# Trainium2 case: VectorE readouts one scan later, ScalarE's side work behind the decays, the D term by transposes, and three GpSimd pairs in the last quarter

## What is computed

```python
xz = einsum('bsd,ed->bse', xn, in_proj_w);  x_in, z = split(xz, 2)
u  = silu(conv4(x_in) + conv_b)                    # 1024 inner channels
dt_r, B, C = split(u @ x_proj_w.T, [64, 80]);  dt = softplus(dt_r @ dt_proj_w.T + b)
# for each token t, state n of 16:
h  = h * exp(dt_t * A) + (dt_t * u_t) * B_t
y  = einsum('bdn,bn->bd', h, C_t)
y  = (y + u * D_param) * silu(z);  out = x + gate * (y @ out_proj_w.T)
```

## Time and profile before

| | |
|---|---|
| time, median of 3 runs | 4975.43 us (4974.64 to 4975.75) |
| the profiled execution's own time | 4976.74 us |
| its span, first to last instruction | 4975.0 us |
| busy, share of the span | PE 89%, DVE 83%, ACT 63%, POOL 81% |
| mean granted TensorE clock | 0.976 of 2.4 GHz |
| first and last `dbu` of GpSimd (L635) | 113.8 and 3733.8 us |

### The profile page before, as it was taken

The page is one execution under the profiler, slowest core; times in us unless marked ns, Lnnn a source line. Parts: engine busy times, 40 slices in busy tenths (PEclk is TensorE's granted clock), DMA queues, the critical chain, the costliest instruction groups (busy, mean ns, idle before and its releaser), DMA issues. The chain is left out here.

```text
span 4975.0 us, 74942 instructions
## 1 busy us (share of the span) xinstructions
PE 4419.1 (89%) x21856; PEld 3161.0 (64%) x21856; DVE 4137.6 (83%) x5011; ACT 3129.7 (63%) x7557; POOL 4010.7 (81%) x1861
## 2 busy tenths in 40 slices
PE   7898888888898989888888888898976999999998
PEld 4666666666666666666666666666654666565664
DVE  2999999999999999999999999999993656566664
ACT  2777777777777777777777777777761333333332
POOL 0999999999999999999999999999992333334332
PEclk9999999999999999999999999999988999999999
DMA  5111111111111111111111111111103323222221
GB/s 193 39 43 46 43 46 43 44 52 52 62 46 44 46 44 46 44 43 44 54 57 58 43 44 46 44 46 43 43 35 112 101 84 100 84 100 79 97 87 45
DMA packets 121581, 301.58 MB, mean 61 GB/s; under 512 B 15394, under 2 KB 20770, under 8 KB 120675
## 3 DMA queue, kind: packets, MB, share of 16 engines
q1 hardware_dynamic: 121186, 296.91, 17.6%
HBM read 245.35 MB, written 51.51 MB: 60 GB/s over the span
## 5 line engine op out<-in xcount | busy, mean ns | idle before, releaser
L635 POOL TENSOR_TENSOR dbu<-du,bc 128x1024 f32<-128x1024 f32 x1024 | 2406.8, 2383 | 111.2 <-DVE du L573 111.2
L396 ACT ACTIVATE dA<-dt,c_A 128x256 f32<-128x256 f32 x4096 | 1753.5, 467 | 524.4 <-DVE hC L539 392.4
L602 DVE TENSOR_TENSOR_SCAN hS<-dA,dbu 128x512 f32<-128x512 f32 x1024 | 1205.4, 1208 | 176.1 <-PE Y L277 123.6
L646 POOL TENSOR_TENSOR hS<-hS,bc 128x1024 f32<-128x1024 f32 x512 | 1220.0, 2383 | 62.7 <-DVE hS L602 62.7
L602 DVE TENSOR_TENSOR_SCAN dA<-dA,dbu 128x512 f32<-128x512 f32 x1024 | 1208.5, 1212 | 20.8 <-ACT dA L396 15.0
L277 PEld LDWEIGHTS Y<-c_ident,hC 128*128 128x128 f32 x4096 | 481.0, 144 | 284.6 <-DVE hC L539 190.2
L277 PE MATMUL Y<-c_ident,hC 128*128 128x128 f32 x4096 | 556.2, 280 | 116.1 <-DVE hC L539 112.1
L539 DVE TENSOR_TENSOR hC<-dA,bc 128x1024 f32<-128x1024 f32 x512 | 627.0, 1225 | 22.4 <-DVE dA L602 5.7
L318 PE MATMUL side<-c_in_w,xnF 128*128 128x512 f32 x1024 | 509.1, 621 | 94.0 <-DVE u L565 55.5
L277 PE MATMUL Y<-c_ident,hS 128*128 128x128 f32 x4096 | 548.9, 278 | 16.1 <-POOL hS L646 16.1
L335 PE MATMUL side<-xnF,c_in_w 128*128 128x256 f32 x2048 | 491.4, 384 | 73.8 <-DVE zs L560 49.1
(11 more groups left out here) (125 smaller groups left out, 5668.5 us busy)
## 6 DMA issues: line engine op xcount, KB each, us to landing
bc<-b_scratch SPq DMA_DIRECT2D x256, 512.0 KB, 3.8
x_in<-in_x SPq DMA_DIRECT2D x32, 512.0 KB, 5.2
o_scratch<-oS SPq DMA_DIRECT2D x64, 256.0 KB, 2.0
p_o_in<-o_scratch SPq DMA_DIRECT2D x32, 512.0 KB, 4.8
p_g_in<-gate_scratch SPq DMA_DIRECT2D x32, 512.0 KB, 5.8
p_x<-in_x SPq DMA_DIRECT2D x32, 512.0 KB, 6.4
x_scratch<-p_x_in SPq DMA_DIRECT2D x32, 512.0 KB, 3.2
p_xr<-x_scratch SPq DMA_DIRECT2D x32, 512.0 KB, 6.8
```

Of the source, the lines that this page charges most:

```text
L396: last = act.activation(dA[:, q % A_RING, e, :], dt[j % 2][:, e, :], ACT.Exp, scale=C["A"][:, 2 * j + e, n:n + 1])
L602: dve.tensor_tensor_scan(out.rearrange("p e t -> p (e t)"), dA[:, q % A_RING, :, :].rearrange("p e t -> p (e t)"), dbu[(q // 2) % B_RING][ ...
L635: gps.tensor_tensor(dbu[p % B_RING][:, :, :, :], du[j % 2][:, :, :].unsqueeze(1).broadcast_to([P, 2, 2, GT]), bc[:, 0, n:n + 2, :].unsquee ...
L646: gps.tensor_tensor(h, h, bc[:, 1, n:n + 2, :].unsqueeze(2).broadcast_to([P, 2, 2, GT]), ALU.mult).then_inc(hcP_done, 1)
```

## The change

It has eight parts.

1. `KINDS` becomes a list by quarter. Quarters 0 to 2 stay GGDGDGDD; quarter 3 becomes GDGDDGDD. A group then has 15 G pairs and 17 D pairs in place of 16 and 16. The slots are still given in turn modulo three, now written out as tables.
2. VectorE reads out a D pair one scan later, behind the first scan of the next pair (`t = 16 * j + 2 * p + 2`).
3. ScalarE goes two units at a time: all four decays of a pair, then the side work of both units.
4. The skip term: ScalarE computes u * D into a new SBUF tile `uD` (`skip_values`, two activations in a quarter, at `UD_AT`), and TensorE adds it by four transposes with the identity. The diagonal matrix and its eight instructions in setup go.
5. The `du` product (L573) is taken out of VectorE's DT step and moved from four units after TensorE's DT piece to five; the copy of dt from six to seven.
6. The XN activations are split in two halves, two units apart; XI copies go from two to three units behind.
7. The sigmoid stages stay one unit apart, and the tables `SIDE`, `D_ACC`, `G_ACC`, `YZ_AT`, `YT_AT`, `YF_AT`, `DMM_AT` and the layer norm's places are new. `YF_AT` of quarter 1 (37) is now below its `YT_AT` (38).
8. VectorE's u product waits for `uD_done` in place of `dmm_done`.

```diff
-KINDS = "GGDGDGDD"
+KINDS = ["GGDGDGDD", "GGDGDGDD", "GGDGDGDD", "GDGDDGDD"]
-D_ACC = [8, 11, 15, 17]
-G_ACC = [7, 10, 14, 17]
+D_ACC = {4: [9, 12, 16, 18], 5: [9, 10, 12, 16, 18]}
+G_ACC = {4: [8, 10, 14, 17], 3: [8, 12, 17]}
@@
-    ("XI", 2, 1, [7, 8, 8, 9]),
-    ("O", 0, -1, [9, 10, 12, 13, 13, 14, 14, 15]),
-    ("CV", 1, 1, [16, 16, 18, 18]),
+    ("XI", 2, 1, [9, 10, 11, 11]),
+    ("O", 0, -1, [10, 11, 11, 11, 12, 12, 13, 14]),
+    ("CV", 1, 1, [15, 15, 16, 17]),
@@
-    ("CV", 0, 2, [57, 58, 59, 60]),
+    ("CV", 0, 2, [57, 59, 60, 61]),
@@
-A_AFTER = {"Z": 2, "CV": 2, "DT": 2, "XN": 2, "XI": 2, "XP": 2, "O": 2}
-DT_COPY = 6
+A_AFTER = {"Z": 2, "CV": 2, "DT": 2, "XN": 2, "XI": 3, "XP": 2, "O": 2}
+S1 = 1
+S2 = 2
+DU_AFTER, DT_COPY = 5, 7
-YZ_AT = [18, 34, 50, 66]
-YT_AT = [20, 36, 52, 68]
-YF_AT = [22, 38, 54, 70]
-DMM_AT = [6, 22, 38, 54]
-Q_STATS, Q_AGGR, Q_RSTD, Q_NMR, Q_XHAT = 34, 35, 38, 40, 42
+YZ_AT = [19, 35, 51, 67]
+YT_AT = [20, 38, 53, 69]
+YF_AT = [23, 37, 56, 70]
+DMM_AT = [8, 24, 40, 56]
+UD_AT = [1, 17, 33, 49]
+Q_STATS, Q_AGGR, Q_RSTD, Q_NMR, Q_XHAT = 29, 31, 34, 34, 38
@@ TensorE, skip_term
-            wait(pe, u_done, g * 4 + (j + 1))
+            wait(pe, uD_done, g * 4 + (j + 1))
-                    last = pe.matmul(Y[:, b, k * P:(k + 1) * P], u[par][:, 2 * j + k, b * P:(b + 1) * P],
-                                     W["skip"][:, 2 * j + k, :], start=(b == 0 and k == 0), stop=False, skip_group_check=True)
+                    last = pe.matmul(Y[:, b, k * P:(k + 1) * P], uD[:, k, b * P:(b + 1) * P], C["ident"][:, :],
+                                     start=(b == 0 and k == 0), stop=False, is_transpose=True, skip_group_check=True)
@@ ScalarE
+        def skip_values(g, j, par):
+
+            wait(act, u_done, g * 4 + (j + 1))
+            wait(act, dmm_done, g * 4 + j)
+            for k in range(2):
+                last = act.activation(uD[:, k, :], u[par][:, 2 * j + k, :], ACT.Copy, scale=C["dcol"][:, 2 * j + k:2 * j + k + 1])
+            last.then_inc(uD_done, 1)
@@
+            for q in range(0, UNITS, 2):
+                if inside(at, 0):
+                    for i in range(2):
+                        bank_freed(act, g, q + i)
+                        if q % NST == 0 and i == 0:
+                            wait(act, dtc_done, g * 4 + (q // NST + 1))
+                        decay(g, q + i, 0)
+                        decay(g, q + i, 1)
+                beside(q)
+                beside(q + 1)
@@ VectorE
-                    if KINDS[p] == "D" and half == 1:
-                        readout(g, j, D_PAIRS.index(p))
                 for j in range(4):
+                    for m, p in enumerate(D_PAIRS[j]):
+                        t = 16 * j + 2 * p + 2
+                        if q == t % UNITS and inside(at, -(t // UNITS)):
+                            readout(g - t // UNITS, j, m)
@@ setup
-        for e in range(KI):
-            dve.tensor_scalar(W["skip"][:, e, :], C["ident"][:, :], C["dcol"][:, e:e + 1], None, ALU.mult)
```

More of the change, by code:

```diff
@@ L102 @@
 S_RING = 3
+C_SLOT = [i % C_RING for i in range(ND)]
+S_SLOT = [(G_BASE[j] + i + sum(j >= at for at in (1, 3)[:-NGP % S_RING])) % S_RING for j in range(4) for i in range(len(G_PAIRS[j]))]
 PAIRS = UNITS // 2
@@ L398, in decay, with simple @@
                 last.then_inc(dA_ready, 1)
-        def simple(kind, j, src, own, par):
+        def simple(kind, j, src, own, par, part):
             wait(act, filled[kind], nth(kind, j, own))
@@ L404, in simple @@
                 wait(act, filled["Z"], own * 4 - 4)
[L405 to L410, removed]
+                for b in range(GB):
+                    k, s = 2 * j + part, (part * GB + b) * P
+                    last = act.activation(xnF[par][:, k, b * P:(b + 1) * P], src[:, s:s + P], ACT.Identity,
+                                          scale=C["gm0"][:, bass.ds(own * GB + b, 1), k], bias=C["bm0"][:, bass.ds(own * GB + b, 1), k])
+                if part == 1:
+                    last.then_inc(xn_done, 1)
             elif kind == "XI":
@@ L480, in stages, with beside @@
                         staged(kind, j, stage, bank[bk], tmp[(sig_base[of] + s) % 2], go + d, earlier(2, s, of, go, sigs_at))
[L482 to L491, removed]
+            def beside(q):
+                stages(q, 2, S2)
+                stages(q, 1, S1)
                 stages(q, 0, 0)
@@ L495, in body @@
                         copy_dt(j, bank[bk], go + d)
-                    if kind in ("XN", "XI", "XP", "O") and q == end + A_AFTER[kind] - off:
-                        simple(kind, j, bank[bk], go + d, (of + d) % 2)
+                    for part in range(2 if kind == "XN" else 1):
+                        if kind in ("XN", "XI", "XP", "O") and q == end + A_AFTER[kind] + 2 * part - off:
+                            simple(kind, j, bank[bk], go + d, (of + d) % 2, part)
                 for j in range(4):
+                    if q == UD_AT[j] and inside(at, 0):
+                        skip_values(g, j, at % 2)
                     t = YF_AT[j]
@@ L561, in side_dve @@
             elif kind == "CV":
-                wait(dve, dmm_done, own * 4 - 8 + (j + 1))
+                wait(dve, uD_done, own * 4 - 8 + (j + 1))
                 wait(dve, filled["XP"], own - 1)
@@ L619, in body @@
                 for (kind, j, d, end, bk, s, off), of, go in side:
+                    if kind == "DT" and q == end + DU_AFTER - off:
+                        step_times_u(j, bank[bk], go + d, (of + d) % 2)
                     if kind in D_AFTER and q == end + D_AFTER[kind] - off:
@@ L652, in body @@
                 for j in range(4):
[L653 to L654 removed]
+                    for m in range(len(G_PAIRS[j])):
+                        t = 8 * j + G_PAIRS[j][m] + G_LAG
                         if p == t % PAIRS and inside(at, -(t // PAIRS)):
@@ L1255, in program @@
             for name, shape in (("in", [P, KD, 2 * DI]), ("x", [P, KI, XD]), ("dt", [XD + 1, DI]),
-                                ("out", [P, KI, D]), ("conv", [P, KI, TAPS, P]), ("skip", [P, KI, P])):
+                                ("out", [P, KI, D]), ("conv", [P, KI, TAPS, P])):
                 const(layer0, W, name + "_w", shape)
```

111 lines of the change are left out of this document (56 added, 55 removed).

## The result

The changed kernel takes 4927.17 us (median, 4924.26 to 4930.41), the kernel before on the same chip 4975.59: ratio 0.9902, 95% interval 0.9885 to 0.9919, so 48 us less. I had forecast 109 us less, 4866. The time lies in my range of 4836 to 4935, near its upper end.

What follows compares the result with a forecast made beforehand. GpSimd was taken as the bound; after the change it needs 109.0 us a group, VectorE 108.8. With 0.9 for unevenness the group takes 110.0; with setup 109.4 us less, 4866 by the median, range 4836 to 4935.

Steps and rivals of the forecast that it cites:

- GpSimd's work: GpSimd's readouts: one fewer a group, 47 instructions in place of 48 at 2.319 us, 74.2 us less work.
- All of it on the path: GpSimd sets the pace, so the 74.2 us of work it loses all come off the kernel's time.
- The boundary wait: First G pair of a group: VectorE's 123.6 us of waits for TensorE's transposes go; 0.85 us a group of jump gap comes.
- ScalarE's waits for decays: VectorE's scans waiting for ScalarE's decays: taken as unchanged at 1.6 us a group, bounds 0 and 5.
- The split XN: XN activations split in halves on ScalarE: said to have units of slack and costed at nothing.
- `take_y` of quarter 1: On ScalarE, ahead of TensorE's turn in order: the place to watch, within the unchanged 1.6 us a group.
- Skip term: ScalarE gains 4 us a group, TensorE saves 2 with no gain in time; price zero, from 0 to 4 us a group.
- Late readout: VectorE's readout one scan later: saves 1.1 us busy time a group; slack before the needing scan falls from 1.24 to 0.10 us.
- my rival on the slower side: Late decays at the scan behind each readout cost 6.2 us a group, some 5025 us; chance of slower 0.12.
- GpSimd's remaining waits: Unevenness of GpSimd and VectorE in turn: 0.9 us a group, 28.8 us in all, where 62.7 are now.
- Setup: VectorE loses 1.65 us of work at setup's end; 1.3 us less time taken, bounds 0 and 1.65.
- VectorE becomes the bound: Rival: slack behind a readout missed in some D pairs, 2.4 us a group, 111.2 a group, around 4904 us; chance 0.17.

Runs made afterwards that it cites:

- the mended one: The changed kernel with XN emptied whole again, two units behind TensorE, and take_y of quarter 1 at unit 39 in place of 37: 4851.03 us, ratio 0.9744.
- four bodies: The changed kernel with XN whole and take_y at 39, plus four bodies in the hardware loop in place of two: 4854.08 us, ratio 0.9756.
- whole XN: The changed kernel with ScalarE emptying an XN bank in one go again, not in two halves two units apart: 4863.12 us, ratio 0.9774.
- the kernel with ScalarE's old order: The kernel before with 15 G and 17 D pairs, TensorE's places for them and the readout one scan later, ScalarE's order as before: 5133.71 us, ratio 1.0313.
- its variant with the matmuls: The changed kernel with XN whole and take_y at 39, skip term by four float32 matmuls with the diagonal matrix, no uD: 4894.25 us, ratio 0.9833.
- the old division: GGDGDGDD in all four quarters, 16 G and 16 D pairs: 4918.45 us in the changed kernel, 4916.06 us with XN whole and take_y at 39.

## Why the prediction was wrong

By its own steps:

- *GpSimd's work.* Right: 1504 instructions, 3487.8 us expected, 3488.9 measured, at the old pitch.
- *"All of it on the path."* Wrong. The 74.2 us count only where nothing else is the bound. In the changed kernel the moved pair is worth nothing (4918 without it, 4927 with it), in the mended one 65 us; in the kernel before it costs 59 (4926 to 4985).
- *The boundary wait.* Right in mechanism: gone, 123.6 to 6.7 us. Its price is 52 us, measured alone. VectorE's own gap at the jump, for which I took 0.85 us a group, is 2.1 us in all; ScalarE's, 3.01 us in the timeline of the result, is the one that VectorE waits for, and four bodies show that it is covered in the mended kernel. The gate `yz`, charged at nothing, waits 17.1 us in all for the transposes, 0.5 a group.
- *ScalarE's waits for decays "unchanged at 1.6 us a group, bounds 0 and 5".* This is the term that failed: 165.4 + 4.4 us, 5.3 a group, above my upper bound. My sentence on the next pair's decays "queued behind each waiting side instruction" has the mechanism, but no price: I had summed how much work stands ahead of a decay, and not what that work itself waits for. With every piece of side work ahead of the next pair's four decays, a wait for TensorE there is a wait of VectorE.
- *The split XN "costed at nothing, units of slack".* Wrong, and the largest single item, 64 us. I counted the slack on ScalarE and forgot its reader: TensorE's XI pieces start at unit 50, and the last half of XN is now written in unit 52.
- *`take_y` of quarter 1.* Named as the place to watch, and priced only inside the 1.6 us. Alone it is 31 us; on top of whole XN it isn't told from nothing.
- *Skip term.* The activation was sized well, 0.497 us against 0.46 and 0.80 as ends, 4.0 us a group. "No gain in time" was wrong: 43 us in the mended kernel (in the changed one it wasn't measured). A busy total of 98 of 109 us says nothing of when its blocks are due.
- *Late readout.* Its mechanism was right, with 0.0 idle ahead of the readout and 1.199 us each. Its slack, which carried my rival on the slower side, showed in full in the kernel with ScalarE's old order, +149 us. In the changed kernel it hardly shows: the scans of D pairs, many of which need slots that a late readout frees, wait 4.4 us for decays in all.
- *GpSimd's remaining waits.* 28.8 us assumed, 79.2 measured. These 50 us are most of the 61 between 4866 and 4927. With the two places mended they are 21.1 in an execution of 4866 us, and the median is 4851, below the forecast.
- *Setup.* 1.3 us less expected; the first `dbu` came 3.3 us later. In the lead-in ScalarE's copy of `xd` starts at 109.79 us in place of 107.03, and the first `dbu` is released by the load `bc<-b_scratch`, where it was `du` before. The new places of XP and XN in TensorE's order stand ahead of that copy; no run parts them.
- *The range and the rivals.* That 4927 lies in the range owes something to luck: two losses that I had at next to nothing (64 and 31 us alone) stand against a gain that I had at nothing (the skip term, 43 us in the mended kernel). It is nearest to the rival "VectorE becomes the bound" (111.2 us a group, 4904; measured 111.8), but not by its mechanism, a slack missed by 0.4 us at six of 17 readouts: the waits for decays of the `hS` scans are 83 of 2.0 us on average, two or three in a group.

By the rule of the Trainium skill ("SBUF — State Buffer", on the shared port pair), contention with GpSimd's reads when both inputs are in SBUF, the moved readout costs GpSimd nothing; GpSimd's pitch, 2.319 us before and 2.320 after, agrees. As to the second rule of the Trainium skill ("TensorE: Matmul & The Clock Gate", on PE-mode transpose), that transposes don't count as busy for the full clock, the mean granted clock did fall, 0.976 to 0.958, but the rows tie the new half-clock stretch to the 3.33 us pause, and it goes with the pause in the kernel with whole XN, which has the same transposes (its mean clock is 0.967 to 0.971). The mended kernel has 0.965 to 0.968 and its variant with the matmuls 0.970 to 0.972; whether the transposes have a part in that small difference stays open.

## What to carry to other kernels

When an in-order engine feeds the bound, each instruction put ahead of the feed must be priced by what it may wait for, not by its duration; look for the reader of every result that is moved later. Work taken off the busiest engine is a gain only as far as the next chain lets it through: test such a move again after the waits are mended. And before a large reordering, see whether the wait that it removes has a small cause of its own, here one ring slot.

## What the runs showed of the hardware

- A pause of 3.33 us in TensorE's work was followed by some six us at the 1.2 GHz level, one of 1.26 us by none; 16 recorded matmuls of 256 columns took 6.67 against 3.69 us.
- GpSimd's recorded duration isn't its cost. The same instruction has a mean record of 2377 ns in the changed kernel, of 2604 in that kernel with the old division, and of 2395 in the mended kernel with the old division. In the last two GpSimd never idles between 1000 and 3000 us, with 864 instructions in both, a pitch of 2.315 us. What sets the length of the record stays open; idle time doesn't. The rows are of these two:

```profile
L667 POOL TENSOR_TENSOR dbu<-du,bc 128x1024 f32<-128x1024 f32 x1024 | 2520.3, 2604 | 113.7 <-DMA bc<-b_scratch 113.7
...
L667 POOL TENSOR_TENSOR dbu<-du,bc 128x1024 f32<-128x1024 f32 x1024 | 2413.0, 2395 | 110.9 <-DMA bc<-b_scratch 110.9
```
